# Layer normalisation of the queries by VectorE, of the contexts by GpSimd, with a signal for each

## The reference

```python
def _inorm(x):
    m = jnp.mean(x, axis=-1, keepdims=True)
    v = jnp.var(x, axis=-1, keepdims=True)
    return (x - m) * jax.lax.rsqrt(v + EPS)
Mn = _conv1x1(Wn, bn, _inorm(x_c))      # x_c: the queries, x
Mm = _conv1x1(Wm, bm, _inorm(x_s))      # x_s: the contexts, ctx
A = softmax(einsum('bct,bcs->bts', Mn, Mm), axis=-1)
Ml = _conv1x1(Wl, bl, x_s)
return _conv1x1(Wo, bo, einsum('bcs,bts->bct', Ml, A)) + x_c
```

## Time and profile before

| | |
|---|---|
| median of 3 runs | 657.51 us (656.33 to 657.82) |
| the profiled execution's own time | 654.93 us |
| its span, first to last instruction | 653.1 us |
| TensorE busy | 579.3 us, 89% |
| VectorE busy | 470.0 us, 72% |
| ScalarE busy | 472.2 us, 72% |
| GpSimd busy | 118.0 us, 18% |
| mean granted TensorE clock | 0.972 |

### The profile page before, as it was taken

One profiled execution on the slowest core, in us unless ns is written; L12 is line 12 of the kernel. 1 busy time (PEld: TensorE's weight loads), 2 busy tenths in 40 slices (PEclk: granted clock), 3 DMA queues, 4 the chain that ended last, 5 costly groups with the idle time before them and its releaser, 6 DMA issues.

```text
span 653.1 us, 25792 instructions
## 1 busy us (share of the span) xinstructions
PE 579.3 (89%) x10867; PEld 507.6 (78%) x10867; DVE 470.0 (72%) x1023; ACT 472.2 (72%) x961; POOL 118.0 (18%) x132
## 2 busy tenths in 40 slices
PE   1689988999799997999799997999989997999975
PEld 1568887978688886988689786888869886888864
DVE  4576777776696966877687766877767776968554
ACT  1589867877588866868587766878668675888571
POOL 3502060100601033100701015100511007000000
PEclk9989999999799998999989998999989999999998
DMA  6302000110020100210010100200002100001000
GB/s 164 131 3 71 2 3 8 66 35 1 3 70 3 34 2 2 71 35 2 2 44 29 34 3 2 70 19 18 2 3 70 35 2 2 3 2 35 3 2 33
DMA packets 18499, 18.32 MB, mean 28 GB/s; under 512 B 1828, under 2 KB 18340, under 8 KB 18404
## 3 DMA queue, kind: packets, MB, share of 16 engines
q1 hardware_dynamic: 18024, 16.55, 8.0%
q0 software_dynamic: 320, 0.26, 0.2%
q10 hardware_dynamic: 60, 0.01, 0.0%
HBM read 12.63 MB, written 4.19 MB: 26 GB/s over the span
## 4 chain that ended last, share of the span: by engine, by line
PE 60%; POOL 11%; DVE 11%; issue 6%; ACT 5%; DVEq 0%; POOLq 0%; ACTq 0%
PE psum L730 8%; PE psum L388 8%; PE psum L676 7%; PE psum L390 7%; PE psum L389 7%; POOL x_norm L1281 5%; PE psum L723 5%; POOL c_norm L1281 4%; PE psum L655 4%; PE psum L640 4%; DVE negmax L1054 3%; DVE shifted L1058 3%; PE psum L543 3%; PE psum L524 2%; POOL rstd L1245 2%
## 5 line engine op out<-in xcount | busy, mean ns | idle before, releaser
L1054 DVE TENSOR_REDUCE negmax<-psum 128x8 f32<-128x512 f32 x128 | 87.3, 682 | 16.0 <-PE psum L655 15.9
L1058 DVE TENSOR_TENSOR shifted<-psum,negmax 128x512 f32<-128x512 f32 x128 | 88.5, 692 | 5.4
L855 ACT ACTIVATE work<-shifted 128x512 f32<-128x512 f32 x128 | 79.0, 629 | 17.8 <-DVE shifted L1058 16.3
L869 ACT ACTIVATE work<-psum,group_mask 128x512 f32<-128x512 f32 x128 | 80.3, 694 | 14.6 <-PE psum L676 14.6
L676 PEld LDWEIGHTS psum<-const,work 64*128 64x128 f32 x1536 | 57.7, 147 | 21.4 <-issue 20.0
L676 PE MATMUL psum<-const,work 64*128 64x64 f32 x1536 | 67.3, 235 | 5.9 <-ACT work L855 4.3
L730 PEld LDWEIGHTS psum<-v,work 128*64 128x64 f32 x2048 | 63.6, 140 | 6.3 <-issue 2.4
L730 PE MATMUL psum<-v,work 128*64 128x34 f32 x2048 | 67.3, 227 | 0.0
L850 ACT ACTIVATE work<-psum,negmax 128x256 f32<-128x256 f32 x128 | 51.7, 486 | 7.9 <-DVE negmax L1050 7.7
L806 ACT ACTIVATE v<-psum 64x256 f32<-64x256 f32 x128 | 49.6, 387 | 9.1 <-PE psum L390 7.8
L1050 DVE TENSOR_REDUCE negmax<-psum 128x2 f32<-128x512 f32 x64 | 42.2, 682 | 14.5 <-PE psum L640 14.5
(11 more groups left out here) (181 smaller groups left out, 1545.6 us busy)
## 6 DMA issues: line engine op xcount, KB each, us to landing
x_raw<-in_x_dram SPq DMA_DIRECT2D x8, 512.0 KB, 4.4
c_raw<-in_ctx_dram SPq DMA_DIRECT2D x8, 512.0 KB, 5.0
out_dram<-attn SPq DMA_DIRECT2D x16, 256.0 KB, 2.7
mrow_u<-in_mask_dram SPq DMA_DIRECT2D x8, 64.0 KB, 5.4
kbd<-in_L_xattn_Wq_dram SPq DMA_DIRECT2D x2, 256.0 KB, 6.7
kbd<-in_L_xattn_Wk_dram SPq DMA_DIRECT2D x2, 256.0 KB, 7.1
kbd<-in_L_xattn_Wv_dram SPq DMA_DIRECT2D x2, 256.0 KB, 7.3
kbd<-in_L_xattn_Wo_dram SPq DMA_DIRECT2D x2, 256.0 KB, 7.7
```

The costliest lines, as they stand in the source:

```text
L855: act.activation(probs[:, exp_row(g, l, i, last), :], shifted[:, i % 2, :], ACT.Exp).then_inc(exps, 1)
L869: act.activation(probsT[:, at, :], o[:], ACT.Copy, scale=group_mask[:, 2 * i + c:2 * i + c + 1]).then_inc(free, 1)
L1054: dve.tensor_reduce(negmax[:, i % 2, :], sv, AX_X, ALU.max, negate=True).then_inc(rowmax, 1)
L1058: dve.tensor_tensor(shifted[:, i % 2, :].rearrange("t (j k) -> t j k", k=C), sv, negmax[:, i % 2, :].unsqueeze(2).broadcast_to([P, NJ, C]) ...
```

## The change

VectorE gets a step XS between S2.3 and V0.0. In it, VectorE waits for `rstd` and normalises the four query blocks, with a signal `x_scaled` of its own. GpSimd keeps the four context blocks, and `normed` now means these alone. Mn waits for `x_scaled`, and Mm gets a wait on `normed`. SP's prefetch waits for both. All other steps keep their order, and the prologue stays as it is.

```diff
 DVE_ORDER = """
-    ST.0 S1.0-7 ST.1 A1.0-1 ST.2 AT1.0 O1.0 A1.2-3 L.2 ST.3 AT1.1 MV.0 O1.1 S2.0-1 L.3 S2.2-3 V0.0-1 Mn.0-1 S2.4-7 Mm.0-1
+    ST.0 S1.0-7 ST.1 A1.0-1 ST.2 AT1.0 O1.0 A1.2-3 L.2 ST.3 AT1.1 MV.0 O1.1 S2.0-1 L.3 S2.2-3 XS.0 V0.0-1 Mn.0-1 S2.4-7 Mm.0-1
...
-NEXT = ("xT", "cT", "nT", "Mn", "Mm", "V0", "K1", "ST", "MV")
+NEXT = ("xT", "cT", "nT", "Mn", "Mm", "V0", "K1", "ST", "MV", "XS")
...
+        x_scaled = sem("x_scaled")
...
                 hold(normed, 1 if g is None else g + 2)
+                if g is not None:
+                    hold(x_scaled, g + 1)
                 hold(mix_ready, 1 if g is None else g + 2)
...
                         if g is None:
                             pe.wait_ge(x_normed, 1)
                         else:
-                            pe.wait_ge(normed, g + 2)
+                            pe.wait_ge(x_scaled, g + 1)
+                    if name == "Mm" and g is not None:
+                        pe.wait_ge(normed, g + 2)
...
+            def normalise_queries(g):
+
+                dve.wait_ge(rstd_ready, g + 2)
+                for p in range(NP):
+                    ins = dve.tensor_scalar(x_norm[:, p, :], x_raw[:, p, :], mean_var[:, p, 0:1], rstd[:, p:p + 1],
+                                            ALU.subtract, ALU.mult)
+                ins.then_inc(x_scaled, 1)
...
+                    elif step[0] == "XS":
+                        normalise_queries(g)
...
-                for t in list(range(NP, 2 * NP)) + list(range(NP)):
-                    src, dst = (x_raw, x_norm) if t < NP else (c_raw, c_norm)
-                    ins = pool.tensor_scalar(dst[:, t % NP, :], src[:, t % NP, :], mean_var[:, t, 0:1], rstd[:, t:t + 1],
+                for t in range(NP, 2 * NP):
+                    ins = pool.tensor_scalar(c_norm[:, t % NP, :], c_raw[:, t % NP, :], mean_var[:, t, 0:1], rstd[:, t:t + 1],
                                              ALU.subtract, ALU.mult)
                 ins.then_inc(normed, 1)
```

More of the change, by code:

```diff
@@ L83, in steps @@
                 out.append((name[0], int(name[1:]), i))
-            elif name in ("H", "L", "SC", "ST", "MV", "WB", "NB", "TG", "NM", "ON", "KB", "OB"):
+            elif name in ("H", "L", "SC", "ST", "MV", "XS", "WB", "NB", "TG", "NM", "ON", "KB", "OB"):
                 out.append((name, i))
```

## The result

The changed kernel takes 633.35 us (median of 4 runs, 632.93 to 635.51) against 656.92 us (653.77 to 657.82): a ratio of 0.9656, 95% interval 0.9616 to 0.9696. Forecast were 635.3 us, range 629.5 to 643. The profiled execution took 633.41 us (span 631.6) where the sum had made 632.7 of the one before.

What follows compares the result with a forecast made beforehand. Bound: all three engines wait before Mn for four GpSimd query instructions. Earlier Mn, 7 x 2.3, plus 6.1 us of clock made 22.2 us: 654.93 to 632.7 us profiled, 635.3 us at the median, range 629.5 to 643.

Steps and rivals of the forecast that it cites:

- The stall as the bound: Before Mn, TensorE, VectorE and ScalarE wait for four GpSimd query instructions of 1.2 us; TensorE stands 24.7 us, seven times.
- Cost of the four instructions: VectorE's four new tensor_scalar between S2.3 and V0: 0.39 us each, 1.4 us for four, bounds 1.1 and 1.9.
- dear end: Upper bound for one new VectorE instruction with two pointer scalars: 537 ns, so four last 1.9 us.
- the copy: SBUF-to-SBUF copy of 64x256 on VectorE, 332 ns, base of the cheap bound: four last 1.1 us.
- Mn's new start: Mn on TensorE starts at 398.55 instead of 400.86, 2.3 us earlier per trip, signal 0.10 us, gap left 1.2 us.
- Clock: TensorE stays at 2.4 GHz with the 1.2 us gap, as no fall followed 1.95 us elsewhere; 6.1 us in total.
- The sum: Whole kernel: 7 x 2.3 + 6.1 = 22.2 us off the profiled 654.93, giving 632.7; 635.3 at the median.
- my template: First trip, 74.43 us to the next Mn at granted 0.99, taken as the model of a full-clock trip.
- A: Rival, chance 0.12: TensorE's clock falls all the same around Mn; gain only 16 us, 641.5 us.
- B: Rival, chance 0.12: VectorE becomes the bound, V0 and mn_lo slip, margin only 0.7 us; gain 15.5 us, 642 us.
- C: Rival, chance 0.03: shared SBUF path holds each new VectorE instruction for one GpSimd instruction, 1.22 us each; slower, 666 us.
- D: Rival, chance 0.01: no effect, because the code waits for something else at Mn.

Runs made afterwards that it cites:

- GpSimd, queries first: Against the changed kernel: GpSimd does both passes again, queries first, each with its own signal, VectorE gets nothing; 622.91 us.
- order alone: Against the kernel before: queries first on GpSimd, but the one signal still behind all eight instructions; one run, 654.73 us.
- half filler: Against the kernel before: 12 useless matmuls on TensorE ahead of the wait before Mn; 651.83 us.
- four behind the signal: Against the changed kernel: four more tensor_scalar on VectorE right behind the signal to TensorE, into a tile nobody reads; 635.11 us.
- the filler: Against the kernel before: 24 useless matmuls of 128x256 on TensorE ahead of the wait before Mn; 646.78 us.

## Why the prediction was right

**The stall as the bound: right.** Removed from its place (GpSimd, queries first), the time goes; left in its place (order alone), it stays.

**Cost of the four instructions: right, by a value between the bounds.** Taken were 0.39 us each and 1.4 us for four; measured 0.406 and 1.37 to 1.38. The dear end, 0.54, was 131 ns too high. The Trainium skill, VectorE: DVE Perf Modes, section Mode 2x_2P, has two elements per cycle for this form. An estimate from the 0.96 GHz of the same page: 256 elements take 133 ns less at two per cycle than at one. Off the dear end's 537 ns that leaves 404, so the row agrees with the rule if each pointer scalar is charged 61 ns as there. Counted from the copy's 332 ns it is 74 ns for both scalars, not 122, so these rows do not settle the price of one. My 0.39 us charged one scalar where the instruction has two; that it came so near is in part luck.

**Mn's new start: right.** 1.33 us of wait instead of 1.2, and a trip of 72.1 us as forecast in the undisturbed ones. The 0.13 us are the signal: I gave it 0.10 us, from `mn_lo`, but from the end of `x_norm` to Mn it took 0.25 us (386.64 to 386.89), as it had behind GpSimd (400.61 to 400.86). Two trips of the first profile lasted 0.7 us longer. In one of them TensorE paused within a row of matmuls, for nothing the profile shows:

```profile
122.07 0.46 PE L728 MATMUL psum<-v,work 128*64 128x65 f32 x9 [0.61 <-issue]
```

In the other no such pause is listed. Pauses of 0.5 and 0.6 us in the same line of matmuls stand in two of the half filler's trips, and in the second profile of the changed kernel the trips are 72.06 to 72.42. I had no term for them; their cause is open.

**Clock: right in the sum, too sure in its reason.** No fall in 21 crossings with a gap of 1.3 us (the changed kernel twice, and with four behind the signal). But my bound, no fall at 1.95 us, came from one gap elsewhere. At Mn, in the profiled executions, falls were 0 of 7 at 0.38 us, 0 of 21 at 1.33, 1 of 7 at 1.82 (probably more in its longer executions), 6 of 7 at 2.62, 6 of 7 at 3.53 with the kernel before, and 6 of 7 at 3.55 with the order alone. At the dear end of my own bounds, 1.9 us for the four, the gap would have been 1.7 us by my sum and 1.9 with the longer signal, and the 18.7 us that I gave for it probably too high. The size, 6.1 us, was under the 6.7 us which the filler gave back in the six intervals alone.

**The sum.** In the profiled executions 21.5 us went, 22.2 were forecast. TensorE's waits give 24.7 - 9.3 = 15.4, the clock in the six intervals 5.3 by my own measure; the two longer trips took 1.4 back. Of the 2.2 us left, 0.4 lie ahead of the first Mn and 1.3 behind the last Mn start, where I had 0.8. The other 0.5 lie in the six intervals: the first trip, my template, was itself 0.2 us longer than the filler's trips (74.43 against 74.18 to 74.21), so 5.3 may be too small. By the filler's 6.7 us the sum would overshoot instead, by 0.9 us in those intervals; no run divides this further.

**The rivals.** A, falls all the same: not with this gap, but at this place they came at 1.8 us (1 of 7 in the profile) and were the rule at 2.6 us (6 of 7). B, VectorE as the bound: no; its margin before `mn_lo` was 0.92 us, not 0.7, and four more instructions made T2.1 0.3 us late per trip. C: the path is shared, but at most 0.23 us was added to one of the four, so the 0.92 us each from which it turns slower are out of reach. The price that I had given, one GpSimd instruction per VectorE instruction, falls. The Trainium skill, SBUF — State Buffer, section Who interferes with whom, calls it an exclusive lock for the whole instruction; for this form the trace does not agree, with 0.1 us more in the median and no hold of 1.2 us. Of my two rows for C, `state_lo` is borne out (0.93 us under the pass, 0.68 clear of it above). The 1226 ns of `norm_bias`, close to one GpSimd product, no run took apart, so for its form a hold of a whole instruction is not excluded. What the 1.24 us of distance protected was little. D, no effect: no; the code waits for the signal at Mn, as the order alone shows.

What I did not see is that the queries could stay on GpSimd: rows 3 had it, since a pass from 390.95 on ends at 395.80, before V0 is done at 397.33.

## What to carry to other kernels

When an engine waits on the last of a batch under one signal, order the batch by its consumers and give each its own signal, before moving work to a faster engine: readiness counts, and a slow engine that is free early beats a fast one that is busy. Price work on a busy engine by which side of the signal it stands on, since four instructions cost some 2 us on one side and 16 on the other. An idle gap of TensorE can cost clock on top, here 1.3 us for each fall; filling it with useless matmuls shows how much.

## What was not expected of the hardware

Matmuls without use made the kernel 8.6 us faster; 6.7 us of it are seen in the six intervals, now at a granted 1.00 throughout. VectorE's fp32 tensor_scalar beside a running GpSimd pass was slowed from 406 to 502 ns in the median and never stopped for long. And TensorE paused for 0.6 us inside a row of matmuls, in some trips and not in others of the same program.
